# Expert loop of a GNN, attention and MoE layer: rows fetched one tile further ahead, all weight loads issued by SyncE

## The reference, cut to what matters

```
def _L0_ffn_ref(x, gate_w, gate_b, w1, b1, w2, b2, gamma, beta):
    gate_logits = x @ gate_w + gate_b                    # 16 experts
    topk_vals, topk_idx = jax.lax.top_k(gate_logits, 2)  # each row goes to 2 of them
    topk_w = jax.nn.softmax(topk_vals, axis=-1)
    h = relu(einsum('bsh,ehf->bsef', x, w1) + b1)        # 256 -> 512
    expert_out = einsum('bsef,efh->bseh', h, w2) + b2    # 512 -> 256
    sel = take_along_axis(expert_out, topk_idx[:, :, :, None], axis=2)
    moe = sum(topk_w[..., None] * sel, axis=2)
    ... layer norm of x + moe
```

## Time and profile before

| | us |
|---|---|
| three runs | 3172.29, 3176.7, 3178.8; median 3176.7 |
| the profiled execution: its time / its span | 3178.54 / 3176.9 |
| expert loop in the span | from 2592 to 3065 |
| TensorE busy over the span | 2696.1 (85%) |
| mean granted TensorE clock, share of full speed | 0.933 |

### The profile page before, as it was taken

One profiled execution on the slowest core, in us unless ns is written; L12 is line 12 of the kernel. 1 busy time (PEld: TensorE's weight loads), 2 busy tenths in 40 slices (PEclk: granted clock), 3 DMA queues, 4 the chain that ended last, 5 costly groups with the idle time before them and its releaser, 6 DMA issues. The chain is left out here.

```text
span 3176.9 us, 47923 instructions
## 1 busy us (share of the span) xinstructions
PE 2696.1 (85%) x14412; PEld 1980.5 (62%) x14413; DVE 1372.2 (43%) x3748; ACT 1363.5 (43%) x2953; POOL 1907.8 (60%) x2005
## 2 busy tenths in 40 slices
PE   0999999999999999888888888898878749989950
PEld 0577667667667666665565665565557738878840
DVE  8655655655655654423222322232227721111138
ACT  4887887887878883000000000000015513333322
POOL 2766666666666665477777777777744742222226
PEclk6999999999999999899988999998989969999975
DMA  7455445445545546766655666666533454353355
GB/s 235 146 169 173 151 158 173 161 148 172 173 133 177 170 139 215 232 184 184 192 179 179 189 185 186 186 186 181 177 89 107 156 161 141 101 176 120 109 178 164
DMA packets 268416, 527.05 MB, mean 166 GB/s; under 512 B 58823, under 2 KB 155086, under 8 KB 268096
## 3 DMA queue, kind: packets, MB, share of 16 engines
q0 software_dynamic: 88848, 240.99, 25.1%
q1 hardware_dynamic: 155312, 259.08, 25.0%
q10 hardware_dynamic: 24064, 24.62, 2.4%
HBM read 394.15 MB, written 131.79 MB: 166 GB/s over the span
## 5 line engine op out<-in xcount | busy, mean ns | idle before, releaser
L725 POOL DMA_INDIRECT pa<-xn_d,srcs x816 | 784.4, 961 | 386.6 <-issue 212.1
L725 POOL DMA_INDIRECT pa<-h_d,srcs x544 | 525.8, 966 | 195.6 <-issue 163.0
L1025 PE MATMUL bank<-t1s,pa 128*128 128x256 f32 x2450 | 608.9, 404 | 0.7 <-DVE scr L1277 0.7
L1025 PE MATMUL bank<-t0s,pa 128*128 128x256 f32 x2450 | 556.0, 384 | 7.3 <-DVE pa L1430 7.1
L1025 PEld LDWEIGHTS bank<-t1s,pa 128*128 128x128 f32 x2450 | 490.2, 205 | 102.4 <-issue 33.1
L1025 PEld LDWEIGHTS bank<-t0s,pa 128*128 128x128 f32 x2450 | 460.6, 191 | 102.4 <-issue 42.8
L1013 PE MATMUL bank<-build 128*128 128x343 f32 x1500 | 466.9, 459 | 63.5 <-DVE build L1412 61.0
L1430 DVE TENSOR_TENSOR pa<-bank,pa 128x343 f32 x750 | 372.6, 512 | 270.3 <-ACT pa L836 126.3
L831 ACT ACTIVATE build<-build,ones 128x343 f32<-128x343 f32 x750 | 436.4, 582 | 24.4
L829 ACT ACTIVATE build<-build,tabs 128x343 f32<-128x343 f32 x750 | 425.1, 567 | 33.0 <-issue 27.4
L1013 PEld LDWEIGHTS bank<-build 128*128 128x128 f32 x1500 | 277.7, 190 | 229.3 <-issue 95.3
(11 more groups left out here) (259 smaller groups left out, 2603.6 us busy)
## 6 DMA issues: line engine op xcount, KB each, us to landing
slab_d<-pa SPq DMA_DIRECT2D x175, 448.0 KB, 5.9
pa<-slab_d SPq DMA_DIRECT2D x175, 448.0 KB, 3.6
pa<-in_w ACTq DMA_DIRECT2D x32, 512.0 KB, 3.9
pa<-in_w SPq DMA_DIRECT2D x32, 512.0 KB, 3.6
pa<-ys_d SPq DMA_DIRECT2D x109, 130.0 KB, 2.1
pa<-xn_d,srcs POOLq DMA_INDIRECT x816
pa<-eo_d SPq DMA_DIRECT2D x49, 256.0 KB, 4.3
pa<-h_d,srcs POOLq DMA_INDIRECT x544
```

What stands on the lines that cost most here:

```text
L725: pool.indirect_dma_start(gath2[b * QT + j], None, table, bass.IndirectOffsetOnAxis(ap=srcs[:, n:n + 1], axis=0)).then_inc(s_g[b], 16)
L1025: ins = pe.matmul(app[i % 2][:, 0:D], slab3[:, s, :], table[:, s * D:(s + 1) * D], start=s == 0, stop=s == T - 1)
```

## The change

SyncE now fetches the rows three tiles ahead, at the head of its turn, and issues the loads of both weights. ScalarE issues none in the loop and reads no expert number. In turn i SyncE reads the row number of tile i+3, waits until the rows of tile i+1 have been copied (`s_e_yT` at i+2; that frees buffer 1-b), loads rows i+3; reads the expert number of tile i+2, waits for `s_e_h` and `s_e_hT` of tile i, loads the first weights; reads the expert number of tile i+1, waits for `s_e_ev` at i (the result of tile i-1 taken), and loads the second weights of tile i+1. The first three row loads and the first two second-weight loads are fitted to this, and the last second-weight load stands behind the loop.

```
             for b in range(2):
                 w1_load(sp, expert(sp, b), b)
+            w2_load(sp, expert(sp, 0), 0)
 ...
             for b in range(2):
                 y_load(slot_row(b), b)
+            row = slot_row(2)
+            sp.wait_ge(s_e_yT, 1)
+            y_load(row, 0)
 
             def e_turn(i, b, n, last):
 
+                if not last:
+                    row = slot_row(i + 3)
+                    sp.wait_ge(s_e_yT, i + 2)
+                    y_load(row, 1 - b)
                 e = expert(sp, i + 2)
-                row = slot_row(i + 2)
-                sp.wait_ge(s_e_yT, i + 1)
-                y_load(row, b)
                 sp.wait_ge(s_e_h, i + 1)
                 sp.wait_ge(s_e_hT, i + 1)
                 w1_load(sp, e, b)
+                e = expert(sp, i + 1)
+                wait_from(sp, s_e_ev, i)
+                w2_load(sp, e, 1 - b)
 
             in_pairs(sp, half - 1, e_turn)
+            e = expert(sp, half * 2)
+            sp.wait_ge(s_e_ev, half * 2 - 1)
+            w2_load(sp, e, 0)
 ...
 (scalar block, e_tile)
                 ins.then_inc(s_e_hT, 1)
-                if not last:
-
-                    e = expert(act, i + 1)
-                    wait_from(act, s_e_ev, i)
-                    w2_load(act, e, 1 - b)
 ...
-            w2_load(act, expert(act, 0), 0)
```

## The result

| | before | changed | ratio (95% interval) |
|---|---|---|---|
| median of 17 runs, us | 3178.25 | 3169.2 | 0.9974 (0.9967 to 0.998) |
| span of the profiled execution, us | 3176.9 | 3169.0 | |
| expert loop, first to last L1254 / L1261 start, us | 465.6 | 453.4 | |

The change brings 0.26%, 8.3 us by the ratio. I had forecast 29. The direction and the range held; the size was more than three times too large. It is rival C of the prediction that came true.

What follows compares the result with a forecast made beforehand. TensorE was taken to bound the loop at 405 us, with 59 us of excess from late rows. 405 + 0 + 22 + 5 + 3 = 435 instead of 464, 29 us less: 3148 us, range 3127 to 3173.

Steps and rivals of the forecast that it cites:

- rival C: Expert loop: weights late instead of rows, changes of expert cost 2.5 to 3.3 us, time 3159 to 3175; chance 0.18.
- What bounds the kernel: Expert loop: TensorE is the bound, 405 us for 108 turns; 59 us of excess, from late rows, can be won.
- Rows three ahead: Head of SyncE's turn: row loads leave 1.5 to 1.9 us after s, and the 8 us lost in plain turns go.
- The added wait in plain turns costs nothing: SyncE, turns without loads: it passes the relu at s + 3.15 and reaches the new wait at s + 4.1, costing nothing.
- A change of expert costs 1.5 us: Expert loop: each of 15 changes costs some 1.5 us instead of 3.4, 22 in all, weights replacing rows.
- the model: The trace's stretch from 2901.42, a change of expert whose steps were worked through, with stalls of 0.7, 0.5 and 0.3 us.
- ready 4.3 after issue: Second weights at a change of expert: issued by SyncE at 2907.7, ready by 2912.0, wanted at 2911.5.
- I add 5: Changes of expert within two to four turns of each other: SyncE hasn't recovered its load time, 5 us added.
- ends, 3: Start and end of the expert loop: together 3 us of the excess remain, bounds 0 and 9.
- SyncE's sum of 416: SyncE's own time in the loop: 107 turns of 3.3 us plus 60 loads of 1.05 us, 416 us.
- D, the slower rival: Weight loads on one queue don't overlap, each takes its full 3.6 us: 13 us slower, 3190; chance 0.10.
- B: Full relief: weights are never late, the loop gains 48 us, time about 3129; chance 0.10.

Runs made afterwards that it cites:

- experiment 5: Kernel before with rows three ahead, second weights still on ScalarE, SyncE also reading the second expert number and waiting, issuing nothing there: ratio 0.9878, loop 434.3 us.
- experiment 7: Changed kernel with half of each weight matrix loaded and used twice: one run 3155.64 us beside 3179.25 for the kernel before, loop 445.4 us.

## Why the prediction was right and wrong

**What bounds the kernel**: right. The row loads set the excess before, TensorE the floor: 404.1 measured with no new weights, 405 worked out.

**Rows three ahead**: right. 8 us of plain turns went, waits for rows went from 53 to 0.1, and alone this edit wins 40 us of loop.

Row loads leave 1.6 and 2.0 after s where nothing is late. Around changes they leave up to 6 after s, and no row wait comes of it: the slack and the stalls for weights cover that.

**The added wait in plain turns costs nothing**: right where SyncE isn't behind. It was too narrow a reading, though. The read and the wait take 0.7 us of rest from each turn, and this rest is what SyncE recovers with after a change; the trace of experiment 5 prices it at 10 to 13 us, its totals don't show it.

**A change of expert costs 1.5 us**: this is the step that failed. The changes that stand alone cost 2.5 to 2.8, the one that I had taken as the model 3.0. With all that comes on top, the loop lies 47.7 over the floor, 3.2 for each of 15 changes, where the sum had 22 + 5 + 3 = 30, 2.0 for each. Three terms were too small:

- SyncE's steps. In turns without a wait, row load to row load takes 3.27 and 3.58 in turn, 3.4 in the mean where I had 3.3. With one load it is 4.4 or 4.8 (I had 4.35 in the mean), with both 5.5 or 5.95 (I had 5.4); there are 26 and 16 such turns, 216 us where I had 200, short waits included. Beside TensorE's 3.73 the rest of a plain turn is 0.3 us, not 0.45, and a change takes longer to recover from.
- The second weights' landing. I took "ready 4.3 after issue". The pair is ready when its bias lands: at the change above issued at 2905.94 and landed 4.8 later, 5.4 after the weights' issue at 2905.37. Two loads overlap there. Of the 16 pairs whose landings the trace has (it lacks the others), 7 leave within 3 us behind first weights and take 5.2 in the median, the 9 others 4.2; before, from ScalarE, it was 5.2 and 4.4. So this belongs to the overlap and not to the queue. A row that I had read had a maximum of 5.4 for this bias, and I used the lone load's time in the one place where loads overlap. It isn't the bound of the loop all the same (experiment 7): with the landings over 1 us shorter, 36 us of holes are left of 42.
- The model followed one change that begins with SyncE on time. From there the first weights left 0.35 later than I had them; then 0.7 of stall was 1.2, and 0.5 was 1.6. The next pair was then on time by the shift, where I had 0.3.

For the first point, the plain turns behind a change: eight row loads on SyncE's timeline, from the start of the first to the end of the last (0.34 long), of which only the last steps hold waits. Seven steps take 24.1 us, 3.45 each:

```profile
2857.58 24.46 SPq L644 DMA_DIRECT2D pa<-ys_d  x8
```

**Sum over close changes, "I add 5", and ends, 3**: about right. 15 changes at the 2.7 of these four are 41, and 7 are left for both.

**SyncE's sum of 416**: short by some 14, which matters since it left a rest of only 19 in a loop of 435. I had written in rival C that this leaves little rest, but priced it as a remnant. 16 of the 42 loaded turns carry both loads, 5.5 us and more against TensorE's 3.73; a prefetch of three microseconds hides that only for a few turns.

**D, the slower rival**: its mechanism isn't there. No load waited for a whole other one, and landings are the same on one queue as on two. **B**: excluded, since weights are late; its 48 us are nearer to the 40 that the rows alone bring, without SyncE's new load. **C**: the mechanism and the size, changes at 2.5 to 3.3 and 3159 to 3175, with 3169.2 measured. (Its own terms, 8 plus 0 to 14 less 2 to 18, give a gain from -10 to 20 and not the 2 to 18 behind that range, so part of the match in size is luck.) I gave it 0.18, when a sum that leaves an in-order engine 96% full should have made it the forecast.

**The Trainium skill's rule** of "DMA: Bandwidth & Descriptors", section "Issuing engines are not separate DMA queues", is that all loads run on the same 16 DMA engines, whichever engine starts them; the trace agrees that the queue doesn't matter to them (the second weights land in 3.8 us from SyncE and in 3.9 from ScalarE). The Trainium skill calls the issue time that a second engine saves, in the same section, "usually small relative to the DMA itself". Measured here, two issues with their branch are 1.05 us beside landings of 3.6 to 3.8, small indeed; but with the reading that goes with them they fill SyncE, and the loop loses 28 to 30 us by it.

## What to carry to other kernels

Split a change that does two things, in the prediction too: here an edit worth 1.1 to 1.2% was cut to 0.26% by its companion. When work moves to an engine that only issues and waits, add up its whole turn with all reads, branches and issues, at the busiest turns and not at the mean; if it is near the pace of the loop, slack of a prefetch delays the loss but doesn't prevent it. A wait's releaser says which transfer came last, not that this transfer was slow: look at when it was issued. And ask for the waits of the engine that issues: if they nearly vanish, it is the bound.

## What the runs showed of the hardware that I had not expected

Halving a load of 512 KB makes it land 1.1 us sooner (3.6 to 2.5 and 3.8 to 2.7), yet won only 6.4 us in 61 loads. Of two DMAs issued 0.55 us apart on one queue, the second landed last in every pair, be it the 512 KB of weights or their bias. The order isn't free: with no other load just ahead, the 128 KB bias lands 3.6 us after its issue behind the weights and 3.8 ahead of them, so it is no faster for going first, while the 512 KB behind it take 4.7 instead of 3.8. A second pair that leaves within 3 us behind first weights is ready 5.2 us after its issue instead of 4.2, from one queue or from two.
